# Products of the convolution written for both heads at once, three transposes in place of five per block, and the second normalization's sums on ScalarE

## The reference, cut to what matters

```python
# x: (8, 256, 512); ctx: (8, 256, 512); 32 heads of 8 rows; L = 512
kv  = einsum('bhil,bhjl->bijhl', ctx, ctx)            # 36 distinct pairs per head, symmetric
y   = causal_conv(kv, ssm_kernel) + kv * D            # along l
a   = einsum('bijhl,bhil->bjhl', y_and_kvD, layernorm(x))
x2  = x + tanh(g0) * a
t   = layernorm(x2)
x3  = x2 + tanh(g1) * (moe(t) + shared_mlp(t))        # 16 experts, top 2, inter 352
```

## Time and profile before

| | before |
|---|---|
| time, median of 3 runs | 746.34 us (744.3 to 748.05) |
| time of the profiled execution | 744.08 us |
| its span | 742.2 us |
| TensorE matmul busy | 716.8 us, 97% |
| VectorE busy | 569.5 us, 77% |
| ScalarE busy | 459.6 us, 62% |
| GpSimd busy | 373.4 us, 50% |
| granted TensorE clock | 1.000 of full speed |

### The profile page before, as it was taken

The page is one execution under the profiler, slowest core; times in us unless marked ns, Lnnn a source line. Parts: engine busy times, 40 slices in busy tenths (PEclk is TensorE's granted clock), DMA queues, the critical chain, the costliest instruction groups (busy, mean ns, idle before and its releaser), DMA issues.

```text
span 742.2 us, 15553 instructions
## 1 busy us (share of the span) xinstructions
PE 716.8 (97%) x4602; PEld 675.0 (91%) x4602; DVE 569.5 (77%) x1111; ACT 459.6 (62%) x659; POOL 373.4 (50%) x190
## 2 busy tenths in 40 slices
PE   3999999999999999999998999999998999999998
PEld 3999999999989999899998999898998999999997
DVE  7899999898955578428888589848996699679942
ACT  7575757575432322126888488858895789678931
POOL 5998888886401065032454334444644454434420
PEclk9999999999999999999999999999999999999999
DMA  7778787877522122563557588766556664432101
GB/s 234 232 228 278 219 271 225 266 225 244 171 100 44 29 43 43 155 170 78 165 162 203 129 238 263 199 174 165 157 134 204 156 193 101 74 68 49 44 1 57
DMA packets 48404, 114.88 MB, mean 155 GB/s; under 512 B 7472, under 2 KB 8624, under 8 KB 48336
## 3 DMA queue, kind: packets, MB, share of 16 engines
q1 hardware_dynamic: 35792, 89.67, 36.6%
q0 software_dynamic: 12544, 24.40, 17.6%
HBM read 157.78 MB, written 29.26 MB: 252 GB/s over the span
## 4 chain that ended last, share of the span: by engine, by line
PE 68%; DVE 12%; DMA 7%; issue 6%; ACT 3%; SPq 3%; ACTq 0%; DVEq 0%; POOLq 0%
PE pair L1288 19%; PE bank L1288 14%; PE pair L1313 12%; PE pair L1224 8%; PE bank L1313 6%; PE bank L1175 4%; DMA out<-ys,slot_info 3%; PE pair L1296 3%; DMA raw<-in_weights 2%; PE bank L1235 2%; SPq L516 2%; DVE prod L819 2%; DVE x L790 2%; DVE bank L824 2%; DVE rows L831 1%
## 5 line engine op out<-in xcount | busy, mean ns | idle before, releaser
L1140 DVE TENSOR_TENSOR w_lo<-raw,w_hi 128x1408 fp32r<-128x1408 f32 x94 | 148.9, 1622 | 46.5 <-ACT w_hi L723 46.0
L1428 POOL DMA_INDIRECT out<-ys,slot_info x47 | 89.2, 1898 | 115.9 <-DMA out<-ys,slot_info 53.9
L1415 POOL DMA_INDIRECT tn<-t_rows,slot_info x47 | 74.1, 1577 | 118.4 <-DVE tT_lo L878 79.5
L723 ACT ACTIVATE w_hi<-raw 128x1408 fp32r x94 | 125.0, 1374 | 10.1 <-DMA raw<-in_weights 7.8
L1224 PE MATMUL pair<-kv_hi,toep_hi 128*128 128x288 f32 x320 | 100.6, 314 | 1.3 <-DMA toep_lo<-kpad_lo 1.3
L1224 PE MATMUL pair<-kv_lo,toep_hi 128*128 128x288 f32 x320 | 95.3, 298 | 0.0
L1224 PE MATMUL pair<-kv_hi,toep_lo 128*128 128x288 f32 x320 | 95.1, 297 | 0.0
L1145 DVE TENSOR_TENSOR w_lo<-raw,w_hi 128x1536 fp32r<-128x1536 f32 x47 | 82.4, 1753 | 10.3 <-ACT w_hi L730 10.3
L1366 POOL TENSOR_TENSOR kv_lo<-kv,kv_hi 128x2304 fp32r<-128x2304 f32 x15 | 77.3, 5151 | 6.0 <-ACT kv_hi L619 6.0
L730 ACT ACTIVATE w_hi<-raw 128x1536 fp32r x47 | 69.3, 1475 | 7.4 <-DMA raw<-in_weights 7.4
L819 DVE TENSOR_TENSOR prod<-pair,q 128x256 f32<-128x256 f32 x128 | 53.5, 418 | 14.8 <-PE pair L1224 9.2
(11 more groups left out here) (221 smaller groups left out, 1978.2 us busy)
## 6 DMA issues: line engine op xcount, KB each, us to landing
raw<-in_weights SPq DMA_DIRECT2D x94, 704.0 KB
raw<-in_weights SPq DMA_DIRECT2D x47, 768.0 KB
toep_hi<-kpad_hi SPq DMA_DIRECT2D x15, 512.0 KB, 4.6
toep_lo<-kpad_lo SPq DMA_DIRECT2D x15, 512.0 KB, 6.2
cx<-in_ctx SPq DMA_DIRECT2D x15, 384.0 KB, 6.3
stage<-in_weights SPq DMA_DIRECT2D x16, 272.0 KB, 6.7
xt<-in_x SPq DMA_DIRECT2D x16, 256.0 KB, 6.4
xr<-in_x SPq DMA_DIRECT2D x16, 256.0 KB, 6.7
```

Source lines behind the costliest of these rows:

```text
L723: act.activation(w_hi[s % 2][:, a:b], raw[:, bass.ds(half + a, b - a)], ACT.Copy).then_inc(hi_ok[n_], 1)
L1140: dve.tensor_tensor(w_lo[s % 2][:, a:b], raw[:, bass.ds(half + a, b - a)], w_hi[s % 2][:, a:b].bitcast(F32), ALU.subtract).then_inc(lo_ok[ ...
L1415: pool.indirect_dma_start(out=tn[o % 2][:], out_offset=None, in_=t_rows, in_offset=bass.IndirectOffsetOnAxis(ap=slot_info[:, 3 * i:3 * i + ...
L1428: pool.indirect_dma_start(out=out, out_offset=bass.IndirectOffsetOnAxis(ap=rows, axis=0), in_=ys[o % 2][:], in_offset=None, bounds_check=R ...
```

## The change

1. `products`: the three multiplications now span both heads (384, 128 and 512 elements per partition in place of 256, 192 and 64 for each head), and wait for the matmuls of both. Most partial products of the 512-wide one go to `ps_rows`. The first addition (512 elements) is as before. A second one adds the upper half of `rows` to the lower half, 256 elements, both inputs and the output in SBUF.
2. `sum_rows`: three transposes in place of five.
3. `q` is laid out by head, with the same two copies. The rows of x and of the output are ordered accordingly by the host.
4. The statistics of x2 go from VectorE to ScalarE, with two passes like those of x. `std_x` moves one tile ahead and to a later place, between the normalization of x and the copy of q.
5. Stage two: unit 1 writes to banks of its own and no longer waits for the hidden product of unit 0, and the last tile's t is turned inside unit 1. The four shared tiles in the middle have a buffer of their own, loaded behind no waiting step. The weight loads are listed one step earlier, with the same waits for the halves of `raw`.

```diff
-PROD_STEPS = 6
+PROD_STEPS = 3
+SUMROWS = 2
...
+MID = [o for o, (routed, i) in enumerate(ORDER) if not routed and LEAD <= o < FINAL[0]]
...
+            if n == 1:
+                return [bank[5], bank[3]]
             return ps_h[1 if n >= FREE_H and n % 2 else 0]
...
             def load_rows(o):
                 routed, j = ORDER[o]
-                if not routed:
+                if not routed and o not in MID:
...
-                if u and u.routed and u.i + 1 < SLOT_TILES - 1:
-                    load_next(u.i + 1, (0, 1))
-                if u and u.routed and 2 <= u.i:
-                    load_next(u.i - 1, (2,))
+                if (s := split_up_at(n)) is not None and s + 1 < SLOT_TILES - 1:
+                    load_next(s + 1, (0, 1))
+                if (s := split_down_at(n)) is not None and s + 1 < SLOT_TILES - 1:
+                    load_next(s + 1, (2,))
+                for o in fills_at(n):
+                    load_rows(o)
+                for k, o in enumerate(MID):
+                    if n == (FIRST_R if k == 0 else last_unit(MID[k - 1]) + 1):
+                        wait(sp, tTl_ok, MID[k - 1] + 1 if k else 0)
+                        sp.dma_start(tn_mid[:], tT_t[ORDER[o][1]]).then_inc(tn_mid_in, 16)
...
+            def stats(src, mv, ok, t):
+                p = t.odd
+                act.activation(spent[:], src[p][:], ACT.Copy, scale=-1.0 / L, accum_out=mv[p][:, 0:1]).then_inc(ok, 1)
+                wait(act, ok, t * 2 + 1)
+                act.activation(spent[:], src[p][:], ACT.Square, bias=mv[p][:, 0:1],
+                               accum_out=mv[p][:, 1:2]).then_inc(ok, 1)
+                wait(act, ok, (t + 1) * 2)
...
             def std_x2(t):
-                wait(act, stat2, (t + 1) * 2)
-                act.activation(sd2[t.odd][:, 0:1], mv2[t.odd][:, 1:2], ACT.Sqrt, bias=small[:, 0:1]).then_inc(std2, 1)
+                wait(act, x2_ok, t + 1)
+                wait(act, rstd2, (t - 1) * 2)
+                stats(x2, mv2, stat2, t)
+                act.activation(sd2[t.odd][:, 0:1], mv2[t.odd][:, 1:2], ACT.Sqrt, bias=small[:, 0:1],
+                               scale=1.0 / L).then_inc(std2, 1)
...
                 if not first and not last:
                     split_kv_hi(t + 1)
-                    std_x(t + 1)
...
                 if not last:
                     norm_x(t + 1)
+                if not t.within(TILES - 2, TILES):
+                    std_x(t + 2)
+                if not last:
                     q_copy(t + 1)
...
-                wait(dve, x2_ok, t + 1)
-                stats(x2, st2, mv2, stat2, t)
...
             def products(t, lb):
...
+                wait(dve, conv_ok, t * 8 + 2 * lb + 2)
+                dve.tensor_tensor(view(w, BATCH, [[n, 2], [HB + BATCH, 3], [1, HB]]),
+                                  view(y, HB, [[512, 2], [HB, 3], [1, HB]]),
+                                  view(z, qo, [[GW, 2], [0, 3], [1, HB]]), ALU.mult).then_inc(prod_ok, 1)
+                dve.tensor_tensor(view(w, 2 * n, [[HB, 2], [HB // 2, 2], [1, HB // 2]]),
+                                  view(y, 4 * HB, [[512, 2], [0, 2], [1, HB // 2]]),
+                                  view(z, qo + HB // 2, [[GW, 2], [HB // 2, 2], [1, HB // 2]]),
+                                  ALU.mult).then_inc(prod_ok, 1)
+                wait(dve, added_rows, t * 4 + lb)
+                dve.tensor_tensor(view(ps_rows, 0, [[HB, 2], [P, 4], [1, HB]]),
+                                  view(y, 0, [[512, 2], [HB, 4], [1, HB]]),
+                                  view(z, qo, [[GW, 2], [BATCH, 4], [1, HB]]), ALU.mult).then_inc(prod_ok, 1)
                 wait(dve, prod_ok, (t * 4 + lb + 1) * PROD_STEPS)
-                dve.tensor_tensor(rows[par][:], ps_rows, prod[par][:, 0:L], ALU.add).then_inc(rows_ok, 1)
+                dve.tensor_tensor(rows[par][:], ps_rows, view(w, 0, [[HB, 4], [n, 2], [1, HB]]),
+                                  ALU.add).then_inc(added_rows, 1)
+                wait(dve, added_rows, t * 4 + lb + 1)
+                dve.tensor_tensor(rows[par][:, 0:SUMROWS * P], rows[par][:, 0:SUMROWS * P],
+                                  rows[par][:, SUMROWS * P:], ALU.add).then_inc(rows_ok, 1)
...
-                for r in range(PRODROWS):
+                for r in range(SUMROWS + 1):
...
-                wait(pe, hid_ok, n if n <= FREE_H else n - 1)
+                if n == 1:
+                    pe.wait_ge(q_ok, 2 * TILES)
+                else:
+                    wait(pe, hid_ok, n if 2 < n <= FREE_H else n - 1)
...
+                    if n == 1 and c == 2:
+                        turn_t(At(TILES - 1))
```

More of the change, by code:

```diff
@@ L353, in tn_count @@
         def tn_count(o):
-            return 16 * sum(ORDER[k][0] == ORDER[o][0] for k in range(o % 2, o + 1, 2))
+            return 16 * sum(ORDER[k][0] == ORDER[o][0] and k not in MID for k in range(o % 2, o + 1, 2))
         def last_unit(o):
@@ L563, in _ @@
             act.activation(small[:, 3:4], small[:, 0:1], ACT.Sqrt)
+            def stats(src, mv, ok, t):
[5 more added lines that the diff above has]
+                wait(act, ok, (t + 1) * 2)
             def std_x(t):
-                p = t.odd
-                wait(act, x_in[p], (t.half() + 1) * 16)
+                wait(act, x_in[t.odd], (t.half() + 1) * 16)
                 wait(act, rstd1, (t - 1) * 2)
[L570 to L575, removed]
+                stats(xt, mv1, stat1, t)
+                act.activation(sd1[t.odd][:, 0:1], mv1[t.odd][:, 1:2], ACT.Sqrt, bias=small[:, 0:1],
                                scale=1.0 / L).then_inc(std1, 1)
             def std_x2(t):
-                wait(act, stat2, (t + 1) * 2)
-                act.activation(sd2[t.odd][:, 0:1], mv2[t.odd][:, 1:2], ACT.Sqrt, bias=small[:, 0:1]).then_inc(std2, 1)
+                wait(act, x2_ok, t + 1)
[3 more added lines that the diff above has]
+                               scale=1.0 / L).then_inc(std2, 1)
             def norm_x(t):
@@ L665, in turn @@
                     std_x(t + 1)
+                if first:
                     split_kv_hi(t + 1)
@@ L691, in tile_hi @@
                     src = ps_t
+                elif o in MID:
+                    act.wait_ge(tn_mid_in, 16 * (MID.index(o) + 1))
+                    act.wait_ge(up_ok, last_unit(o - 2) + 1)
+                    src = tn_mid
                 else:
@@ L765, in _ @@
             dve.tensor_tensor(krow_lo[:], krow[:], krow_hi[:].bitcast(F32), ALU.subtract).then_inc(krowl_ok, 1)
-            def stats(src, st, mv, ok, t):
-                p = t.odd
-                dve.bn_stats(st[p][:], src[p][:]).then_inc(ok, 1)
-                wait(dve, ok, t * 2 + 1)
-                dve.tensor_copy(hop[:, 1:2], hop[:, 0:1])
-                dve.bn_aggr(mv[p][:, 0:2], st[p][:]).then_inc(ok, 1)
             def scale_x(t):
@@ L830, in products @@
-                wait(dve, prod_ok, (t * 4 + lb + 1) * PROD_STEPS)
-                dve.tensor_tensor(rows[par][:], ps_rows, prod[par][:, 0:L], ALU.add).then_inc(rows_ok, 1)
+                y, z, w = ps_conv[par][:], q[t.odd][:], prod[par][:]
+                qo, n = lb * 2 * GW, 4 * HB
+                wait(dve, summed, t * 4 + lb - 1)
+                if lb == 0:
+                    wait(dve, q_ok, (t + 1) * 2)
+                wait(dve, conv_ok, t * 8 + 2 * lb + 2)
+                dve.tensor_tensor(view(w, BATCH, [[n, 2], [HB + BATCH, 3], [1, HB]]),
+                                  view(y, HB, [[512, 2], [HB, 3], [1, HB]]),
+                                  view(z, qo, [[GW, 2], [0, 3], [1, HB]]), ALU.mult).then_inc(prod_ok, 1)
@@ L1232, in sum_rows @@
                 wait(pe, rows_ok, t * 4 + lb + 1)
-                for r in range(PRODROWS):
-                    part = (rows if r < BLOCKS else prod)[lb % 2]
-                    mm = pe.matmul(ps_o[:, lb * P:(lb + 1) * P], part[:, r * P:(r + 1) * P], ident[:],
-                                   is_transpose=True, start=(r == 0), stop=(r == PRODROWS - 1))
+                last = prod[lb % 2][:, 8 * HB:]
+                for r in range(SUMROWS + 1):
+                    part = rows[lb % 2][:, r * P:(r + 1) * P] if r < SUMROWS else last
+                    mm = pe.matmul(ps_o[:, lb * P:(lb + 1) * P], part, ident[:],
+                                   is_transpose=True, start=(r == 0), stop=(r == SUMROWS))
                 mm.then_inc(summed, 1)
@@ L1492 @@
     got = run(nc, [arrays], core_ids=[0]).results[0]["out_0"]
-    return got.reshape(TILES, HD, 2, BATCH, L).transpose(3, 0, 2, 1, 4).reshape(BATCH, HEADS * HD, L)
+    return got.reshape(TILES, 2, HD, BATCH, L).transpose(3, 0, 1, 2, 4).reshape(BATCH, HEADS * HD, L)
```

48 lines of the change are left out of this document (11 added, 37 removed).

## The result

| | before | after |
|---|---|---|
| time, median | 746.77 us (744.3 to 748.41, 6 runs) | 807.9 us (797.55 to 815.2, 6 runs) |
| ratio | | 1.0767, 95% interval 1.0728 to 1.0806 |
| profiled execution | 744.08 us | 807.02 us |
| its span | 742.2 us | 805.2 us |
| granted TensorE clock, mean | 1.000 | 0.972 |

The change makes the kernel 7.7% slower. The time lies in the predicted range of 766 to 812 us, but not where the forecast put it, at 778: it is close to what the first rival gave, 804. Whether that rival's mechanism is what happened has to be read turn by turn.

A forecast was written before the change was run, and what follows sets the result against it. Stage one was taken as a ring through TensorE, ScalarE and VectorE, with VectorE's addition held by GpSimd. 744.08 + 27.2 + 8.7 - 1 - 3 = 776.0 us for the profiled execution, 778 for the median; range 766 to 812 us.

The forecast's parts named there:

- the first rival: Stage one: kv_lo starts before block 0's addition, every second turn takes 18.3 us, 26 us more, 804 us; chance 0.27.
- The last addition is held behind GpSimd: Stage one: the 256-element addition with two SBUF inputs stands until GpSimd's instruction is through, ending 0.27 us after it.
- A turn of 14.3 us with block 1 held: Tiles 2 to 14: block 1's addition waits for kv_lo; turns of 14.3 us against 12.21, +27.2 us over 13 turns.
- The addition of block 0 is 0.33 us ahead and goes through: Each stage-one turn: block 0's addition asks at 3.67 us, before kv_lo starts at 4.00, and isn't held.
- the delay that products 3 hand on: Stage one: block 2's held addition delays products 3 by 0.2 to 0.3 us, eating the 0.33 us margin in some turns.
- A long turn has 18.3 us: Stage one: if kv_lo wins, block 0's addition ends at 9.42 us, sum 1 at 13.9, and the turn is 18.3 us.
- First turns, +8.7: Start of stage one: held additions cost 5 us in the first turn and 3.7 in the second, together +8.7 us.
- Stage two, -4: Stage two: -1 us at its start, for waits of unit 1, and -3 us from SyncE's list.
- The term of the SyncE list, -3: Stage two: without queueing behind the load of rows, TensorE's 1.92 us wait and later ones go; -3 us, bounds 0 and -4.
- Statistics and the two-head products at nothing: Stage one: statistics on ScalarE cost nothing, hidden by the kv_lo wait; products over both heads got no term in the sum.
- The unheld case, 743.6: Rival for stage one: the addition isn't held, turns take 12.3 us, 743.6 us, no change or just faster; chance 0.10.
- the ring through VectorE: Stage-one turn without a hold: products 3 and 0, residual, sums, conv 2 and conv 3 in sequence, 12.3 us.

The follow-up runs named there:

- the pair of 821 and 766 us: Kernel before plus one unneeded 256-element addition per block: both inputs in SBUF 821.07 us (ratio 1.0984), one input in PSUM 765.89 us (1.0258).
- the folding in PSUM: Changed kernel with three additions of 256 elements, each with one input in PSUM, in place of one of 512 and one of 256: 751.43 us, ratio 1.0051.

## Why the prediction was right in its mechanism and off in its number

- *The last addition is held behind GpSimd.* Right, and shown by the pair of 821 and 766 us and by the folding in PSUM. It ends 0.28 us after GpSimd's, predicted 0.27. One premise was put too widely: not every VectorE instruction of stage one had an input in PSUM (the statistics at L770 read SBUF alone), but none in the turn read two inputs from SBUF.
- *A turn of 14.3 us with block 1 held.* Right for the turns it describes: 14.14 to 14.4 us, the addition of block 1 standing 2.3 to 2.5 us. 13 of these are 184.5 us against 159.3 before (12.26 a turn), which is +25.2, predicted 27.2.
- *The addition of block 0 is 0.33 us ahead and goes through.* This is the step that failed, in five of the 13 turns. The lead measured 0.28 us where nothing delayed it. The rival had the right place, and its reason, the delay that products 3 hand on, was the whole reason in one long turn of the five (0.29 us). In the other four the race was lost by the branch of the loop, 0.27 to 0.33 us of "issue", which the prediction didn't count. The trace of before doesn't show it: from the third turn on VectorE waits 0.36 to 0.40 us for q ahead of products 0, and the branch is hidden in that. In the new ring it waits no more, and the branch is on the path. Without it the profiled execution had no long turn.
- *A long turn has 18.3 us.* Mis-sized: 19.66 on the mean. The term that was missing is TensorE's clock, conv 2 in 4.27 us for 2.45. Five long turns at 5.47 more are 27.4 us; the rival had 6.5 of them at 4.0, which is 26. Two misses cancel, and its 804 comes near 808 partly by luck.
- *First turns, +8.7.* Measured +11.1 (48.45 against 37.34 us for the third copy of q): 5.0 for the first turn as estimated, 6.1 for the second where 3.7 was predicted. In that one, too, the granted clock fell, to 0.57 from 40 to 44 us.
- *Stage two, -4.* Measured -1.6 with the clock low at its start (+1.5), and -2.2 by itself. The term of the SyncE list, -3, was too hopeful: waits for weights of 2.7 us in three places remain, against 3.5 in four before, and a wait of 1.8 us for a hidden product, at 294.30, is new.
- *Statistics and the two-head products at nothing.* Right: 749.0 and 745.6 us.
- *The unheld case, 743.6.* Without the hold the kernel that keeps the folding has 751.4, not 743.6: the ring through VectorE was put at 12.3 us and is 12.6 on the mean. Of the difference, 0.15 us is the branch (turns of 12.77 with it and 12.47 without) and about 0.16 the third addition of this form of the folding, in the two blocks that the ring holds. Without the folding it is 745.6.

The accounting for the profiled execution: 11.1 (first turns) + 25.2 (13 turns at the short length) + 27.4 (five long ones) + 0.9 (to the start of stage two) - 1.6 = 63.0, and 805.2 - 742.2 = 63.0.

What stays open: when the clock falls. With the loop written out TensorE waits 0.72, 0.26 and 1.61 us in a turn and keeps its full clock in all turns. With kv_lo in four pieces it waits 0.63 and 1.51 and loses it. With kv_lo held back until block 0 is done, turns with waits of 0.64, 0.68 and 1.90 us keep it, and turns with 0.72, 0.25 and 1.89 lose it. The longest wait doesn't tell them apart, and no run here was made to settle it. Nor is it shown what spreads the executions of the kernel without the branch over 16 us.

## What to carry to other kernels

Before moving work onto VectorE beside a busy GpSimd, look at where each operand lies: an operand in PSUM costs its own time, two in SBUF cost whatever is left of GpSimd's instruction, which can be ten times as much. Where two engines race for something that is held for 5 us, a margin of 0.3 us is no margin: count into it the branches and the delays that a block hands on to the next, expect every second turn to differ, and give the time of a turn for either outcome. And a wait of TensorE can cost twice, since the matmuls behind it may run at half the clock; look at the granted clock of a stretch before explaining its length by waits alone.

## What the runs showed of the hardware that was not expected

- The branch of a two-turn loop shows on VectorE as 0.26 to 0.34 us of "issue" ahead of the first instruction of the body. Writing the loop out took 18 us off the median here (807.9 to 789.9); the profiled execution shows the race behind it won in every turn.
- TensorE's granted clock fell from 2.4 to 1.2 GHz in turns in which it was busy for most of the time and idle for at most 1.51 us at once (kv_lo in four pieces), and in one kernel (kv_lo after block 0) in every second turn alone.
- Saving transposes on TensorE bought nothing in any form: 0.76 us less work per turn (751.4 us), 0.22 less in one block (745.0), none less (745.0).
